# Gate weights loaded through ScalarE's DMA queue instead of SyncE's

## The reference

```python
query  = ctx @ Wq.T + bq;  key = ctx @ Wk.T + bk
attn   = softmax(query @ key.T)                   # per batch, 256 x 256
x      = x + layernorm(x) mixed over its last axis by attn
h      = layernorm(x)
gate   = silu(bit_linear(h, gate_w, gate_b))      # 256 -> 1024
val    = bit_linear(h, val_w, val_b)              # 256 -> 1024
out    = x + bit_linear(gate * val, out_w, out_b) # 1024 -> 256
```

## Time and profile before

| what | us |
|---|---|
| median of 3 runs | 60.81 |
| lowest and highest | 60.74, 60.81 |
| the profiled execution's own time | 61.23 |
| its span in the trace | 59.5 |

### The profile page before, as it was taken

How to read it: one execution, slowest core, us unless ns; L and a number is a source line. 1 busy time by engine, 2 the same in 40 slices (tenths; PEclk the granted TensorE clock), 3 DMA queues, 4 the chain that set the end, 5 groups by cost and what they waited for, 6 DMA issues and landing times.

```text
span 59.5 us, 1140 instructions
## 1 busy us (share of the span) xinstructions
PE 51.0 (86%) x298; PEld 32.6 (55%) x301; DVE 48.3 (81%) x122; ACT 47.6 (80%) x84; POOL 45.0 (76%) x102
## 2 busy tenths in 40 slices
PE   1999993999999699929899988899999998889910
PEld 1768842958888478713323634333473753669800
DVE  3249858887999899997998989898999997997150
ACT  0723927999999999978999684999999999698700
POOL 4970006199789888798879978989999999999900
PEclk9999999999999999999999999999999999999999
DMA  0687989999995000000002000399170199920573
GB/s 0 167 305 285 339 315 392 408 406 414 398 409 219 4 6 11 0 6 0 6 0 44 0 0 15 73 174 178 40 147 0 23 184 180 237 81 0 176 232 121
DMA packets 11069, 8.92 MB, mean 150 GB/s; under 512 B 7604, under 2 KB 9140, under 8 KB 11064
## 3 DMA queue, kind: packets, MB, share of 16 engines
q1 hardware_dynamic: 10912, 8.72, 47.4%
q10 hardware_dynamic: 152, 0.14, 0.9%
HBM read 6.04 MB, written 1.05 MB: 119 GB/s over the span
## 4 chain that ended last, share of the span: by engine, by line
POOL 30%; PE 30%; issue 19%; DVE 10%; ACT 5%; POOLq 0%; ACTq 0%
POOL h L344 6%; PE psG L763 5%; PE psO L940 5%; PE psT L778 5%; PE psT L753 5%; POOL r_cols L276 4%; PE psV L763 4%; PE psH L940 3%; POOL rstd L311 3%; ACT o_early L723 3%; DVE x L485 3%; POOL pgam L325 2%; DVE nmax L467 2%; POOL res L372 2%; POOL w_int L409 2%
## 5 line engine op out<-in xcount | busy, mean ns | idle before, releaser
L572 DVE TENSOR_REDUCE pmax<-prod 128x1 f32<-128x1024 f32 x8 | 9.7, 1210 | 0.1
L707 ACT ACTIVATE sil<-psG,s_gv 128x1024 f32<-128x1024 f32 x8 | 8.9, 1111 | 0.6 <-PE psG L874 0.2
L556 DVE TENSOR_TENSOR prod<-psV,sil 128x1024 f32<-128x1024 f32 x7 | 8.5, 1221 | 0.9 <-ACT sil L707 0.5
L859 PE MATMUL psG<-ter_gate,hT 128*128 128x512 bf16 x31 | 8.0, 378 | 0.8 <-ACT sil L707 0.7
L886 PE MATMUL psV<-ter_val,hT 128*128 128x512 bf16 x26 | 7.0, 382 | 0.2 <-issue 0.2
L940 PE MATMUL psO<-ter_out,pT 128*128 128x256 bf16 x48 | 6.2, 272 | 0.7 <-ACT o_early L723 0.7
L940 PEld LDWEIGHTS psO<-ter_out,pT 128*128 128x128 bf16 x48 | 4.4, 98 | 2.4 <-DVE pT L599 0.8
L694 ACT ACTIVATE hT<-psH,unshift 128x256 bf16<-128x256 f16 x8 | 3.8, 474 | 1.5 <-PE psH L842 1.4
L859 PEld LDWEIGHTS psG<-ter_gate,hT 128*128 128x128 bf16 x32 | 2.7, 96 | 4.0 <-issue 2.0
L664 ACT ACTIVATE p_int<-prod,pqs 128x1024 int16<-128x1024 f32 x4 | 4.6, 1141 | 0.0
L715 ACT CAST pT<-pT_int 128x1024 bf16<-128x1024 int16 x4 | 4.2, 1038 | 0.5 <-DMA pT_int<-p_int 0.5
(11 more groups left out here) (142 smaller groups left out, 145.3 us busy)
## 6 DMA issues: line engine op xcount, KB each, us to landing
w_gate<-in_w_gate SPq DMA_DIRECT2D x2, 512.0 KB, 5.5
x<-in_x_tok SPq DMA_DIRECT2D x4, 256.0 KB, 7.1
w_val<-in_w_val SPq DMA_DIRECT2D x2, 512.0 KB, 7.3
xt_sb<-in_x_T SPq DMA_DIRECT2D x4, 256.0 KB, 7.9
w_out<-in_w_out SPq DMA_DIRECT2D x2, 512.0 KB, 8.9
out_x<-res SPq DMA_DIRECT2D x8, 128.0 KB, 1.8
ctx_sb<-in_ctx_T SPq DMA_DIRECT2D x2, 128.0 KB, 2.8
ctx_sb<-in_ctx_T SPq DMA_DIRECT2D x1, 256.0 KB, 6.8
```

Source lines behind the costliest of these rows:

```text
L556: nc.vector.tensor_tensor(prod[:, t % P_RING, :], psV[:], sil[:, t % S_RING, :], ALU.mult).then_inc(prod_done, 1)
L572: nc.vector.tensor_reduce(pmax[:, t:t + 1], prod[:, t % P_RING, :], AX.X, ALU.max, apply_absolute_value=True).then_inc(pmax_done, 1)
L707: nc.scalar.activation(sil[:, t % S_RING, :], psG[:], ACT.Silu, scale=s_gv[:, t, 0:1]).then_inc(sil_done, 1)
L859: nc.tensor.matmul(psG[:, c * HC:(c + 1) * HC], hT[:, t, k, :], w_ter[0][:, k * HID + c * HC:k * HID + (c + 1) * HC], start=(k == 0), stop ...
```

## The change

SP's list loses `load_w(0, 0)` and `load_w(0, 1)`, the two halves of the gate weights. ACT issues the same two transfers with the same semaphores, after the bias rows and before its function table's load. The order of SP's other loads stays, and so does every wait.

```diff
-            load_ctx(0, 0, 1); load_ctx(1, 1, 2); load_w(0, 0); load_x(0, 0, 2); load_w(0, 1);
+            load_ctx(0, 0, 1); load_ctx(1, 1, 2); load_x(0, 0, 2);
             load_ctx(2, 2, 4); load_x(1, 2, 4); load_x(2, 4, 6); load_x(3, 6, 8); load_w(1, 0);
...
             act.dma_start(bh_sb[:], b_hidden).then_inc(l_bh, 16)
+            for z in range(2):
+                act.dma_start(w_sb[0][:, z * HALF:(z + 1) * HALF], w_gate[z]).then_inc(l_w[0][z], 16)
             act.wait_ge(c_fill, 2)
```

## The result

| | before | changed |
|---|---|---|
| executions, us | 60.81, 60.81, 60.74, 61.07 | 61.63, 64.84, 62.09, 66.54 |
| mean granted TensorE clock | 1.00 (profiled) | 0.999, 0.946, 1.000, 0.921 |
| median, us | 60.81 | 63.47 |
| ratio of executions at full clock | | 1.017 (1.0113 to 1.0227) |

The changed kernel is slower, at full clock by 1.1 to 2.3%. The ratio leaves out the two executions whose clock fell, and without them the median of 63.47 can't be understood. So there are two effects to explain: 1.0 us in executions at full clock (forecast 0.3), and a clock that falls in two of the four executions.

A forecast was written before the change was run, and what follows sets the result against it. It took two tied paths to bound the kernel: PE's chain of waits and ACT's row behind the gates' second half. A landing 0.4 us later, less 0.1 slack, gave 60.81 + 0.3 = 61.1 us; range 60.2 to 61.8.

The forecast's parts named there:

- Issue time on ACT and SP: Two issues before ACT's table load, 0.85 us hidden by idle time, cost nothing; SP's loads issued 0.4 to 0.9 earlier, gain nothing.
- Who stands ahead of the second half: DMA queues at the gates' second half: SP's packets share the engines, so it lands 0.4 us later, at 9.65.
- nothing in it can shrink: ACT's work behind the gates' second half: a later landing moves the whole row, here by 0.4 us.
- The row with equal counts: Trace stretch with 90 ACT-queue and 83 SP packets; one-for-one service puts 256 KB more ahead of the second half, 0.8 us.
- A fuller stream: DMA from 3.5 to 9.3 us: idle engines find work in the second queue, 0.4 us earlier on ACT, 60.4; chance 0.34.
- The old order again: DMA queues alternate by whole transfers, so the gates land as before, 0 us, 60.8; chance 0.18.
- The rule of whole packets in turn: DMA engines go round queues by packets; gates, x piece and context alternate as before, sum nearer 0 than 0.3 us.
- The second rule: Issuing engines: a second one saves only issue time, which here would be a gain of nothing.
- A larger share for SP: DMA queues: 128 ACT packets to SP's 204 delay the second half 1.7 us, 62.4, or 63.1 by bytes; chance 0.09.

The follow-up runs named there:

- the gates alone: Changed kernel, but SP waits for the gates' first half before issuing x piece 0 and all behind it; one execution, 62.47 us.

## Why the prediction was wrong

- *Issue time on ACT and SP.* Right. The table load ends at 4.0 and ACT is idle another 0.77 ahead of its first k copy; 0.83 us of issues cost nothing. SP's earlier issue brought nothing: the value weights' first half is issued 2 us earlier, at 4.32, and lands no sooner (8.8 us after it, at 13.1).
- *The step that failed.* The prediction priced the second half only. It wrote that the halves now share the engines with SP's packets, and drew from this nothing for the first half, which has `k_out(1)` behind it on ACT and PE's energies behind that. It landed 1.65 us later (7.85 for 6.2), and between 8.2 and 8.5 in other profiles. A step that walks each moved load to its first reader, and that reader's successors, would have found it. Part of the working was at hand: by equal counts x piece 0's 256 KB pass with the first half, 0.8 us, from the first half's landing at 6.2 to 7.0, and `k_out(1)` starts 0.7 later than it did. The measured delay is twice that.
- *Who stands ahead of the second half: 0.4.* A mis-sized term. ACT's sum started 0.64, 0.84, 1.02 and, with 20 matmuls added on PE, 1.24 later in four profiles with both halves on ACT's queue beside SP's loads. The row with equal counts gave 0.8, near the middle of these; the choice of 0.4 had a reason, but no row for its size. The way from there to the end was partly misread: "nothing in it can shrink" was said of ACT's row, and 0.2 us of it did. At full clock 0.4 arrives at the end of the profiled execution and about 0.9 in the median with the copy of k put first.
- *Signs that came true, and luck.* The second half's sum (9.93), the first exponential 1.05 behind it, the table load and POOL's row at 21.68 are as forecast, and so is the profiled execution's 61.63 beside 61.5. The third batch's projections are not (10.67, forecast before 10.02), nor is the idle time ahead of that sum (0.50, forecast 1.7 to 2.2). These two show the first half's path, which sets the reciprocal in this execution. That the number fits is luck, since both paths happened to move by the same 0.4.
- *The clock.* Not in the prediction at all, and it makes the median 63.47. The runs point to the idle stretch ahead of batch 1's energies. Made without the second queue, it comes with low clocks in 4 of 6 executions, and with half of it filled in 2 of 6 on the same chip. With the copy of k put first, which moves the stretch and shortens it, there are none in 6, beside 3 of 6 on the same chip. Filled whole there are none in 12, but on another chip. It raises the chance of a fall and doesn't decide it alone.
- *A fuller stream* (0.34). Fell. Two queues moved fewer bytes in the first 4 us, 1.09 for 1.22 MB. The sign I gave for it, a DMA share over 0.93, was a bad one: the second profile of the changed kernel has 0.96 and 312 GB/s from 3.5 to 9.3. The share counts the time in which packets are in work, and an equal share can carry fewer bytes.
- *The old order again* (0.18). Fell as well. The transfers landed in pairs. The rule of whole packets in turn, in the Trainium skill's "DMA: Bandwidth & Descriptors", section "Queues, rings and completion order", was read by me as an alternation that keeps the old order. A pair that lands together at 7.4 and 7.85 shows a finer sharing, or turns that begin with x. The second rule, in the same page of the Trainium skill, section "Issuing engines are not separate DMA queues", that a second issuer saves only issue time, holds for the gain, which was none, and leaves out the loss.
- *A larger share for SP* (0.09). Seen in the counts for a while, 128 packets to 68 from 3.5 to 5.5 us, and then no more, 106 to 109. The delay of 1.7 that it gave for the second half didn't come.

Open: why the stream is slow up to about 7.5 us in all kernels (260 to 322 GB/s from 3.5 to 7.5 us, against 397 to 412 from 9.3 to 13.3 in all but the gates alone), and how far its order or the side-by-side service makes the loss at full clock. Open too is what makes the first half's delay twice the estimate. Also open is how the idle stretch and the fall of the clock are tied in detail: by the one profile of each kernel, stretches of 1.44, 1.76 and 1.89 us had low clocks in 1, 3 and 2 of 6 executions, and those of 1.51 and 1.82 in none. In all but one of these kernels the profiled execution was one at full clock, so a stretch as it was ahead of a fall has been seen once.

## What to carry to other kernels

A queue served in order is a priority list, and taking a transfer out of it gives up its place: here two transfers in two queues landed together, at about the later time. Before moving a load, follow both its reader and the instructions behind that reader on the same engine, for every part of the load. And look at what TensorE would wait for: an idle stretch of some 2 us early in this kernel cost 0.4 us by its chain in one profile, and 2 to 5 us where the clock fell.

## What the runs showed of the hardware

- Two DMA queues in use moved 1.09 MB from 3.5 to 7.5 us, one queue 1.22 MB; with the same share of the engines' time (mean of both windows: 54.1% and 30.6% for the two queues, 84.1% for the one). In the other profiles it was 260 to 272 GB/s with two queues, and 298 in one of them, and 292 to 322 with one.
- A transfer's landing rose from 4.5 to 6.8 us after issue with its own queue, place and issue time unchanged, when another of 512 KB was put in the other queue; alone, in either queue, it was 4.5 to 4.6.
- The granted clock was at 0.50 from 12.0 to 18.5 us while PE was busy throughout. It fell 1.4 us after PE had resumed from an idle stretch of 1.89. With twenty or twenty-four small matmuls (0.12 us each) in the stretch, none of 12 executions had a low clock.
